# A four-layer graph network on one core: plain, relational and graph layers put into one program per engine, their first products taken tile by tile

## The chip, the cores and the metric

The kernel runs on one core of one Trainium2 chip. The metric is the device time of one launch in microseconds. The core has five instruction streams: TensorE (PE, matrix products; PEld is its weight load), VectorE (DVE), ScalarE (ACT), GpSimd (POOL) and SyncE (SP, which here only issues transfers). They meet through semaphores. PEclk is the TensorE clock that was granted, as a share of 2.4 GHz.

## The reference, cut to what matters

A graph of 3125 nodes and 100000 edges, 128 features a node, goes through four blocks. Ahead of each stands a layer norm with relu, behind each a residual sum.

```
h = relu(layernorm(x)); x += L0(h): relational max over incoming edges, relu
h = relu(layernorm(x)); x += L1(h): relu(bn((h + sum of h[src]) @ W1)) @ W2, relu     (the "plain" layer)
h = relu(layernorm(x)); x += L2(h): twice  out = sum over edges of (h @ W[rel])[src] + h @ loop_w + b
h = relu(layernorm(x)); x += L3(h): h @ W_in + b_in, then four times
        t = h @ Wc[i]; agg = sum of t[src] * norm + bc[i]; h = layernorm(h + relu(agg)) * g + b
```

## The kernel before, in words

The nodes are 25 tiles of 128. The first stage (until 1213 us of the profile) computes L0 and beside it counts the edges into adjacency matrices, in 8 bits: one plain matrix (25 strips of 400 KB) and one split by relation (32 halves of 1600 KB). From then on the edge sums are matrix products of such a strip with the node rows. The rows are cut into a high and a low 16-bit part, so each (tile, strip) pair costs two products. A "cut" is such a pair of parts: `g.zcut` lies in the tile Z, `g.cut` in the tile cut.

After it come three blocks. Each is a `nc.Block()` with one program for each engine, and at its end the engines meet in a barrier:

- `isomorphism_layer`, the plain layer. Five rounds of five tiles. A round is 100 products on PE (line 1269: 50 of 384 columns, 50 of 256), the hidden product (line 1287) and the second product (line 1299). DVE and ACT normalise the round and write its cut (`GroupNorm`, lines 832 to 860; its semaphore `s_cut` rises by 2 a round). SP loads the plain strips, then the first four relational halves, and stores each round's cut to the DRAM table from which POOL gathers (line 1229).
- `relational_layers`, two passes of 32 halves. On PE a half is 50 products of 512 columns (`dense`, line 1853), in between lie the gathered sums (`few`, line 1835) for the nine sparse tiles and the tile products (`tile`, line 1811). POOL gathers rows for `few` (line 1575). SP issues seven parameter loads at the start (line 1581), then the halves (line 1589), each when its slot is free, then the plain strips 0 to 19 (line 1593). DVE waits for all seven transfers and reduces them to statistics (lines 1674 to 1679). PE transposes these (line 1865) between its first and its second half. The last pass makes the inputs of the graph layers tile by tile, in an order called `order`: `again` (line 1820, a transpose) and `enter` (line 1825, the product with W_in) lag two tiles behind, so two of each stand after the loop. DVE ends it with the cut of the last tile (line 1664).
- `graph_layers`, four layers of five rounds. A round is again 100 products (line 1269) and five products with the weights (line 1299); DVE normalises. SP loads the weights (line 1429) and the last five strips (line 1431). PE and DVE begin when the weights have landed (lines 1447 and 1498).

The order of work is written out by hand in each engine's program; each queue runs its own instructions in that order.

Of the kernel before, what the change touches and what calls it, by code (L numbers as in the profile page):

```python
# [23 lines left out]
ALU = mybir.AluOpType  # L24
# [1208 lines left out]
class Sums:  # L1233
# [24 lines left out]

    def tensor(self, e, i, cut, weights, base=0, parts_of=None):

        g, n = self.g, base * (2 * TROUNDS)

        def sums(q, tiles):
            last, (lo, hi) = None, self.parts[q]
            for a in tiles:
                adj = g.arena[:, i * TILES * NT * P // 4:(i + 1) * TILES * NT * P // 4].bitcast(F8).rearrange(
                    "p (k a n) -> p k a n", k=TILES, a=NT)[:, lo:hi, a, :]
                for part in range(2):
                    last = e.matmul(self.sums(i, q), cut[:, a, part, :], adj, start=a + part == 0,  # L1269
                                    stop=a + part == NT)  # L1270
            return last
# [7 lines left out]
        for q, (lo, hi) in enumerate(self.parts):  # L1279
# [3 lines left out]
            sums(q, range(NT - TILES, NT) if i == 0 and parts_of else range(NT)).then_inc(self.s_sum, 1)  # L1283
        for q, (lo, hi) in enumerate(self.parts):
# [53 lines left out]
def isomorphism_layer(g):  # L1338
# [7 lines left out]
    with g.nc.Block() as block:  # L1346
        @block.gpsimd
        def _(e):
            e.sem_inc(m.s_go, 1)

        @block.sync
        def _(e):
            load_adjacency(g, e, s_ld)

            def half(k):
                e.wait_ge(m.s_sum, 2 * ((4 * k + 3) // TILES + 1))
                e.dma_start(*load_half(g, k, k)).then_inc(s_half[k], 16)

            def rows(r):
                e.wait_ge(norm.s_cut, 2 * (r + 1))  # L1360
                store_cut(g, e, g.zcut, r, s_row)
            half(0)
            rows(0)
            half(1)
            rows(1)
            half(2)
            rows(2)
            half(3)
            rows(3)
            rows(4)  # L1370

        @block.vector
        def _(e):
            step = Chain(e, s_c)
            batch_norm_vector(g, e, step, s_v, s_r)
            for i in range(TROUNDS):
                for q, (lo, hi) in enumerate(m.parts):
# [12 lines left out]
        def _(e):  # L1390
            batch_norm_scalar(g, e, s_v, s_r)
            for i in range(TROUNDS):
                m.scalar(e, i, 1.0 / (scale * COUNT))
                norm.scalar(e, i)
# [766 lines left out]
```

## Time and profile before

| | us |
|---|---|
| median of three runs | 2650.6 (2649.99 to 2651.94) |
| the profiled execution | 2652.58, span 2650.7 |
| PE busy | 1977.3 (75%) |
| DVE busy | 1328.0 (50%) |
| POOL busy | 1490.7 (56%) |
| ACT busy | 670.7 (25%) |
| mean granted clock of PE | 0.808 |
| plain layer | 1214.6 to 1308.3 |
| relational layers | 1308.7 to 2321.4 |
| graph layers | 2321.9 to 2640.6 |

The spans of the layers are from the first to the last instruction of each in the timeline. In 40 equal slices of the span (66 us each), PE and its clock read:

```profile
PE   6744545555554545436899999998999999799996
PEclk8855655656565655568999999999999999899998
```

A digit is a tenth of a slice. From the 20th slice on PE is busy nearly all the time at full clock; the dip near the end is where the relational layers end and the graph layers begin.

### The profile page before, as it was taken

The page shows a single profiled execution, that of the slowest core. Times are in us where ns is not written, and L with a number is a line of the kernel's source. Part 1 is how long each engine was busy: PE and PEld are TensorE (multiplying, and loading weights), DVE is VectorE, ACT ScalarE, POOL GpSimd, SP SyncE. Part 2 cuts the span into 40 slices and gives each one's busy share as a digit, 9 for nine tenths or more (in the row PEclk, how much of TensorE's full clock was granted, in tenths as well). Part 3 has the DMA queues.
Part 4 walks back from the last instruction along what each step waited for, and adds up shares of the span by engine and source line. Part 5 has one row for each costly group of instructions (what it writes and reads, how often), then busy time and mean ns, then how long its engine had stood idle before and what let it go on. Part 6 is the DMA issues. An engine that isn't in the chain of part 4 may idle for free. (4 is left out here: it accounts for less than half of the span.)

```text
span 2650.7 us, 33489 instructions
## 1 busy us (share of the span) xinstructions
PE 1977.3 (75%) x11712; PEld 1095.3 (41%) x11712; DVE 1328.0 (50%) x3186; ACT 670.7 (25%) x1332; POOL 1490.7 (56%) x1528
## 2 busy tenths in 40 slices
PE   6744545555554545436899999998999999799996
PEld 3411111111121111124555555554555555467775
DVE  6466666666666666654322222221323332357775
ACT  4244445445454444424200000000000000100000
POOL 4277777777777777760156666663576657400000
PEclk8855655656565655568999999999999999899998
DMA  5545555555555555564354454465444444610000
GB/s 177 184 130 159 168 166 160 172 157 162 157 162 156 162 165 168 156 203 166 129 172 160 148 171 150 150 144 144 163 149 161 131 161 147 104 40 1 1 6 21
DMA packets 183331, 370.18 MB, mean 140 GB/s; under 512 B 38760, under 2 KB 119254, under 8 KB 174838
## 3 DMA queue, kind: packets, MB, share of 16 engines
q1 hardware_dynamic: 129208, 263.74, 28.1%
q0 software_dynamic: 48704, 101.21, 16.4%
q10 hardware_dynamic: 5246, 3.03, 0.4%
q8 instruction: 96, 1.57, 0.2%
q14 instruction: 77, 0.63, 0.1%
HBM read 232.54 MB, written 135.28 MB: 139 GB/s over the span
## 5 line engine op out<-in xcount | busy, mean ns | idle before, releaser
L925 POOL DMA_INDIRECT arena<-table_rel,key_rel x784 | 789.0, 1006 | 278.0 <-issue 233.6
L1053 PE MATMUL ps_out<-arena 128*128 128x400 f16 x1024 | 380.4, 509 | 438.2 <-DVE arena L959 396.6
L1097 ACT ACTIVATE arena<-ps_out 128x800 fp8e4<-128x800 f32 x512 | 400.2, 834 | 437.1 <-PE ps_out L1053 436.9
L1575 POOL DMA_INDIRECT arena<-table_cut,src_at x324 | 312.6, 965 | 277.2 <-DMA table_cut<-Z 111.7
L943 DVE SCALAR_TENSOR_TENSOR arena<-arena,keep_max 128x128 f32<-128x128 f32 x784 | 275.3, 351 | 328.5 <-DMA arena<-table_rel,key_rel 318.6
L1575 POOL DMA_INDIRECT arena<-table_next,src_at x324 | 314.9, 972 | 186.6 <-issue 91.8
L1053 PEld LDWEIGHTS ps_out<-arena 128*128 128x128 f16 x1024 | 85.3, 117 | 656.4 <-DVE arena L959 409.6
L1853 PE MATMUL ps_out<-arena,Z 128*128 128x512 fp8e4 x1600 | 352.3, 380 | 0.0
L1853 PE MATMUL ps_out<-arena,cut 128*128 128x512 fp8e4 x1600 | 350.2, 379 | 0.0
L959 DVE TENSOR_TENSOR arena<-iota,arena 128x1072 f16<-128x1072 f16 (+1 forms) x384 | 271.5, 707 | 0.0
L1269 PE MATMUL ps_out<-arena,cut 128*128 128x384 fp8e4 (+1 forms) x1500 | 207.9, 300 | 45.3 <-PEq L116 43.5
L1853 PEld LDWEIGHTS ps_out<-arena,Z 128*128 128x128 f16 x1600 | 156.8, 98 | 183.6 <-issue 2.2
L1853 PEld LDWEIGHTS ps_out<-arena,cut 128*128 128x128 f16 x1600 | 156.5, 98 | 182.7
L1835 PE MATMUL ps_out<-arena 128*128 128x256 f16 x1296 | 166.1, 283 | 34.5 <-issue 26.3
L1269 PEld LDWEIGHTS ps_out<-arena,cut 128*128 128x128 f16 x1500 | 147.1, 98 | 103.7 <-issue 47.5
L1835 PEld LDWEIGHTS ps_out<-arena 128*128 128x128 f16 x1296 | 127.5, 99 | 68.5 <-issue 28.5
L1040 PE MATMUL ps_t<-arena 128*128 128x50 f16 x1568 | 96.6, 212 | 77.7 <-DVE arena L953 77.7
L1617 DVE TENSOR_SCALAR CS<-ps_out,unit 128x512 f32<-128x512 f32 x32 | 24.0, 751 | 256.8 <-PE ps_out L1853 256.8
L1617 DVE TENSOR_SCALAR CS<-ps_out 128x512 f32<-128x512 f32 x32 | 22.1, 692 | 260.1 <-PE ps_out L1853 260.1
L1040 PEld LDWEIGHTS ps_t<-arena 128*128 128x128 f16 x1568 | 87.6, 118 | 139.2 <-DVE arena L953 92.1
L1269 PE MATMUL ps_out<-arena,Z 128*128 128x384 fp8e4 (+1 forms) x1000 | 139.5, 302 | 7.2 <-DMA w<-in_L_gnn_bc 6.3
L1777 ACT ACTIVATE tT<-ps_t 128x128 f32<-128x128 f32 x50 | 13.4, 268 | 517.9 <-PE ps_t L1785 517.9
(312 smaller groups left out, 1993.8 us busy)
## 6 DMA issues: line engine op xcount, KB each, us to landing
arena<-adjacency SPq DMA_DIRECT2D x64, 1600.0 KB, 7.0
adjacency<-arena SPq DMA_DIRECT2D x160, 320.0 KB
running_rows<-arena SPq DMA_DIRECT2D x392, 128.0 KB
arena<-adjacency_plain SPq DMA_DIRECT2D x50, 400.0 KB, 9.4
table_rel<-arena SPq DMA_DIRECT2D x25, 512.0 KB, 2.9
arena<-table_rel,key_rel POOLq DMA_INDIRECT x784, 2.9
adjacency_plain<-adj SPq DMA_DIRECT2D x50, 128.0 KB, 2.5
arena<-table_cut,src_at POOLq DMA_INDIRECT x324
```

The costliest lines, as they stand in the source:

```text
L925: e.indirect_dma_start(message(t), None, table, bass.IndirectOffsetOnAxis(key[:, t:t + 1], 0)).then_inc(s_msg[t % both], 16)
L943: e.scalar_tensor_tensor(fold(t), fold(t - 1), g.keep_max[:, t:t + 1], message(t), ALU.add, ALU.max).then_inc(s_run, 1)
L959: e.tensor_tensor(*onehot(g.hot_spot, b % 2, first, end, g.spot, b)).then_inc(s_spot, 1)
L1040: e.matmul(out[:, :, w * WIN:(w + 1) * WIN], g.hot_low[:, q % 2, w // 2, :, w % 2], g.hot_flat[:, q % 2, w // 2, :, w % 2].rearrange("p (a ...
L1053: last = e.matmul(g.ps_out[:, u % 2, x * 512:x * 512 + KW], g.hot_low[:, q % 2, k, :, x], g.hot_spot[:, b % 2, k, :, x], start=True, stop= ...
L1097: e.activation(g.half[h % 2].rearrange("p (a w x) -> p a w x", a=NT, x=R * WIN)[:, :, at:at + 2, :], g.ps_out[:, u % 2, 0:1024].rearrange( ...
L1269: last = e.matmul(self.sums(i, q), cut[:, a, part, :], adj, start=a + part == 0, stop=a + part == NT)
L1575: e.indirect_dma_start(g.picked[:, w % 2 * BLOCKS + k, :, :].rearrange("p a f -> p (a f)"), None, tables[y], bass.IndirectOffsetOnAxis(g.s ...
L1617: e.tensor_scalar(rows[:, k % 2, :, h * HD:(h + 1) * HD].rearrange("p r (w n) -> p r w n", n=WIN), g.ps_out[:, h, 0:512].rearrange("p (w r ...
L1777: e.activation(g.tT[:, i % 2, :], g.ps_t[:, i % 2, 0:P], ACT.Copy).then_inc(s_hT, 1)
L1835: last = e.matmul(g.ps_out[:, w % 2, 1024:1024 + CODES], g.picked[:, w % 2 * BLOCKS + k, part, :], g.hot_code[:, w % 2, k // 2, :, k % 2], ...
L1853: last = e.matmul(g.ps_out[:, h, 0:512], cuts[y][:, a, part, :], adj[:, a, :], start=x + part == 0, stop=x + part == NT)
```

## The change

The three blocks become one block with one program per engine. `isomorphism_layer` and `graph_layers` no longer open blocks; they return their four programs (SP, DVE, ACT, PE), and `later_layers` (formerly `relational_layers`) calls the plain layer's ahead of its own and the graph layers' behind it. Waits on semaphores stand where the meetings were:

- PE: the plain layer, then `dense(0, 0)`, which now waits for each round's cut (`norm.s_cut`) before the first product on that round's tiles. The first transpose `turn(0)`, which wrote a bank that the plain layer used, moves behind it. The order of the rest of the passes stays.
- PE, end of the second pass: the 50 products of the first graph round's first part (384 columns) are made in `early`, in the tile order `order`, each waiting for that tile's cut (`s_late`), between the two last `again` and the two last `enter`; then the 50 of 256 columns. `products` is the rest of the round, split from `tensor`.
- SP: the relational parameters wait for the plain layer's last product, behind that layer's last store. The graph weights wait for the last tile product, the last five strips for the last gathered sum.
- DVE waits for the plain layer's last sums before it writes `codes` over the strips; ACT waits for the plain layer's last rows; POOL needs only the five stores, as before.

```diff
+    def add(self, e, i, q, cut, tiles, begin, end):
+        g, last, (lo, hi) = self.g, None, self.parts[q]
+        for x, a in enumerate(tiles):
+            ...
+            for part in range(2):
+                last = e.matmul(self.sums(i, q), cut[:, a, part, :], adj, start=begin and x + part == 0,
+                                stop=end and x + part == len(tiles))
+        return last
...
-def graph_layers(g, a, out, s_plain):
+def graph_layers(g, a, out, s_plain, s_p, s_sum):
...
+    def sync(e):
+        e.wait_ge(s_p, 2 * NT)
+        for part in params:
+            e.dma_start(*part).then_inc(s_par, 16)
+        e.wait_ge(s_sum, 2 * GATHERED)
+        for k in range(NT - TILES, NT):
+            e.dma_start(g.slot(k, NT * P, U8), g.adjacency1[k]).then_inc(s_last, 16)
...
             for i in range(TROUNDS):
+                if n == 0 and i == 0:
+                    e.wait_ge(s_par, 16 * len(params))
+                    m.products(e, 0, g.w9[:, 0:D])
+                    continue
...
         @block.sync
         def _(e):
+            before[0](e)
+            e.wait_ge(iso.s_prod, 2 * TROUNDS)
             for part in params:
                 e.dma_start(*part).then_inc(s_par, 16)
...
+            behind[0](e)
...
         @block.vector
         def _(e):
+            before[1](e)
...
+            e.wait_ge(iso.s_sum, 2 * TROUNDS)
             codes(0, 0)
...
+            behind[1](e)
         @block.scalar
         def _(e):
+            before[2](e)
+            e.wait_ge(norm.s_h, NT)
             e.wait_ge(s_deg, 1)
...
                 for x, a in enumerate(order if y and m == 0 else range(NT)):
                     if y and m == 0:
                         e.wait_ge(s_ready, x + 1)
+                    elif m == 0 and a % TILES == 0:
+                        e.wait_ge(norm.s_cut, 2 * (a // TILES + 1))
...
-            turn(0)
+            before[3](e)
             for y in range(2):
                 for m in range(HALVES + 1):
                     if m < HALVES:
                         dense(y, m)
                     if y == 0 and m == 0:
+                        e.wait_ge(iso.s_read, 2 * TROUNDS)
+                        turn(0)
                         e.wait_ge(s_stat, 1)
...
-            for i in range(NT, NT + 2):
-                again(i)
-                enter(i)
-    return s_plain
+            def early(lo, hi):
+                for x in range(lo, hi):
+                    e.wait_ge(s_late, x + 1)
+                    done = last.add(e, 0, 0, g.zcut, order[x:x + 1], x == 0, x == NT - 1)
+                return done
+            e.wait_ge(s_ev, 2 * HALVES)
+            e.wait_ge(s_plain[0], 64)
+            e.wait_ge(s_plain[1], 64)
+            early(0, 10)
+            again(NT)
+            early(10, 14)
+            enter(NT)
+            early(14, 18)
+            again(NT + 1)
+            early(18, NT - 2)
+            enter(NT + 1)
+            early(NT - 2, NT).then_inc(last.s_sum, 1)
+            e.wait_ge(s_o2, NT)
+            last.add(e, 0, 1, g.zcut, order, True, True).then_inc(last.s_sum, 1)
+            behind[3](e)
```

First place, PE from the plain layer's last products (1299 before, 1306 now) to the second half of the first pass (1853 before, 1865 now). Before:

```order
L1299 MATMUL ps_t<-w,CS 128x128 x5
L1346 UNCONDITIONAL_BRANCH
L1779 UNCONDITIONAL_BRANCH
L1785 MATMUL ps_t<-ident,tin 128x128
L1853 MATMUL ps_out<-arena,Z 128x512 x50
L1865 MATMUL ps_out<-ident,stat 1x128 x3
L1853 MATMUL ps_out<-arena,Z 128x512 x50
```

And now:

```order
L1306 MATMUL ps_t<-w,CS 128x128 x5
L1865 MATMUL ps_out<-arena,Z 128x512 x50
L1795 MATMUL ps_t<-ident,tin 128x128
L1879 MATMUL ps_out<-ident,stat 1x128 x3
L1865 MATMUL ps_out<-arena,Z 128x512 x50
```

The first 50 products follow the plain layer with no meeting between; the transpose of tin moved behind them; the three transposes of stat keep their place ahead of the second 50.

Second place, PE from the last tile product of the second pass (1811 before, 1821 now) to the first weights product of the graph layers (1299 before, 1306 now). Before:

```order
L1811 MATMUL ps_out<-w,tT 128x128
L1825 MATMUL ps_out<-tH 128x128
L1820 MATMUL ps_out<-ident,CS 128x128
L1825 MATMUL ps_out<-tH 128x128
L1820 MATMUL ps_out<-ident,CS 128x128
L1825 MATMUL ps_out<-tH 128x128
L1562 UNCONDITIONAL_BRANCH
L1496 UNCONDITIONAL_BRANCH
L1269 MATMUL ps_out<-arena,Z 128x384 x50
L1269 MATMUL ps_out<-arena,Z 128x256 x50
L1299 MATMUL ps_t<-w,CS 128x128 x5
```

And now:

```order
L1821 MATMUL ps_out<-w,tT 128x128
L1835 MATMUL ps_out<-tH 128x128
L1265 MATMUL ps_out<-arena,Z 128x384 x20
L1830 MATMUL ps_out<-ident,CS 128x128
L1265 MATMUL ps_out<-arena,Z 128x384 x8
L1835 MATMUL ps_out<-tH 128x128
L1265 MATMUL ps_out<-arena,Z 128x384 x8
L1830 MATMUL ps_out<-ident,CS 128x128
L1265 MATMUL ps_out<-arena,Z 128x384 x10
L1835 MATMUL ps_out<-tH 128x128
L1265 MATMUL ps_out<-arena,Z 128x384 x4
L1265 MATMUL ps_out<-arena,Z 128x256 x50
```

The 50 products of 384 columns now stand among the last `again` (1820, now 1830) and `enter` (1825, now 1835), and only the last four are behind the last `enter`.

Third place, SP around the parameter loads. Before:

```order
L1229 DMA table_cut<-Z 128x5x256 x2
L1346 UNCONDITIONAL_BRANCH
L1578 UNCONDITIONAL_BRANCH
L1581 DMA w<-in_L_gnn_W 128x8x128
```

And now:

```order
L1229 DMA table_cut<-Z 128x5x256 x2
L1584 DMA w<-in_L_gnn_W 128x8x128
```

The loads stay behind the store of the last round's cut.

## Rows read from the trace of the kernel before

**Rows 1.** The chain that ended last, in order of time: start, duration, what.
```profile
2321.83 0.05 issue
...
2322.31 4.22 DMA w<-in_L_gnn_bc
...
2326.57 15.63 PE ps_out L1269 x100
...
2343.57 13.58 PE ps_out L1269 x100
```

**Rows 2.** Waits of PE, 1322 to 2289 us: total, times, longest.
```profile
PE ps_out L1835 <- issue: 14.6, 5, 7.6
PE ps_out L1835 <- DVE arena L1606: 8.2, 4, 2.7
```

**Rows 3.** Timeline at the first meeting: start, duration, instruction, [idle before, releaser].
```profile
1297.12 1.38 PE L1299 MATMUL ps_t<-w,CS 128*128 128x128 f32 x10 [0.23 <-ACT CS L1316]
...
1309.46 0.48 PE L1785 MATMUL ps_t<-ident,tin 128*128 128x128 f32 x1 [10.96 <-ACT tin L1764]
...
1309.73 12.70 PE L1853 MATMUL ps_out<-arena,Z 128*128 128x512 fp8e4 x50
...
1313.61 31.50 SPq L1589 DMA_DIRECT2D arena<-adjacency  x4
...
1319.56 1.35 DVE L1675 TENSOR_REDUCE stat<-w 128x1 f32<-128x1152 f32 x1 [7.26 <-DMA bias<-in_L_gnn_ln_b]
...
1321.16 0.29 DVE L1677 TENSOR_REDUCE stat<-tH 128x1 f32<-128x128 f32 x1
...
1322.27 0.49 PE L1865 MATMUL ps_out<-ident,stat 128*1 128x128 f32 x3
...
1322.59 10.96 PE L1853 MATMUL ps_out<-arena,Z 128*128 128x512 fp8e4 x50
```

**Rows 4.** The SP queue of its own at the first meeting.
```profile
1307.96 0.37 SPq L1229 DMA_DIRECT2D table_cut<-Z  x1
1308.73 0.37 SPq L1581 DMA_DIRECT2D w<-in_L_gnn_W  x1
```

**Rows 5.** Stretches: busy time and count by engine, granted clock, DMA share, GB/s.
```profile
1290.00:1300.00 10.00, 8.27 (x66) 6.59 (x63) 3.26 (x6) 2.04 (x4) 0.00 (x0) 1.00 0.11 33
1305.00:1310.00 5.00, 0.54 (x2) 0.36 (x3) 2.87 (x7) 1.67 (x7) 0.00 (x0) 0.50 0.22 60
...
2305.00:2309.00 4.00, 3.98 (x18) 2.40 (x18) 0.00 (x0) 0.00 (x0) 0.00 (x0) 0.50 0.27 107
2309.00:2313.00 4.00, 3.37 (x16) 3.37 (x17) 0.48 (x1) 0.66 (x3) 0.00 (x0) 0.50 0.01 4
2313.00:2316.00 3.00, 0.95 (x7) 0.76 (x6) 1.80 (x9) 0.59 (x2) 0.00 (x0) 0.94 0.00 0
```

**Rows 6.** Transfers issued 1308 to 1322 us: count, KB, us to landing.
```profile
arena<-adjacency SPq DMA_DIRECT2D x1, 1600.0 KB, 10.7
...
bias<-in_L_gnn_ln_g SPq DMA_DIRECT2D x1, 256.0 KB, 5.3
bias<-in_L_gnn_ln_b SPq DMA_DIRECT2D x1, 256.0 KB, 6.4
```

**Rows 7.** Timeline at the second meeting.
```profile
2304.98 4.00 PE L1835 MATMUL ps_out<-arena 128*128 128x256 f16 x18 [11.06 <-issue]
...
2313.56 0.39 PE L1825 MATMUL ps_out<-tH 128*128 128x128 f32 x2
...
2316.16 0.33 PE L1820 MATMUL ps_out<-ident,CS 128*128 128x128 f32 x1 [2.21 <-ACT CS L1749]
...
2318.10 0.49 ACT L1749 ACTIVATE CS<-X,small,inv_dev 128x128 f32<-128x128 f32 x1 [0.43 <-DVE small L1657]
...
2319.49 0.79 PE L1825 MATMUL ps_out<-tH 128*128 128x128 f32 x2 [0.37 <-ACT tH L1755]
...
2321.03 0.35 DVE L1664 SCALAR_TENSOR_TENSOR Z<-H,dsc,Z 128x128 f16<-128x128 f32 x1
```

More of the change, by code:

```diff
@@ L1283, in tensor, with products @@
             sums(q, range(NT - TILES, NT) if i == 0 and parts_of else range(NT)).then_inc(self.s_sum, 1)
+        self.products(e, i, weights, base)
+    def products(self, e, i, weights, base=0):
+        n = base * (2 * TROUNDS)
         for q, (lo, hi) in enumerate(self.parts):
@@ L1403, in isomorphism_layer, with half, rows @@
-    return s_row, s_half
-def graph_layers(g, a, out, s_plain):
+    def sync(e):
+        load_adjacency(g, e, s_ld)
+        def half(k):
+            e.wait_ge(m.s_sum, 2 * ((4 * k + 3) // TILES + 1))
+            e.dma_start(*load_half(g, k, k)).then_inc(s_half[k], 16)
+        def rows(r):
+            e.wait_ge(norm.s_cut, 2 * (r + 1))
+            store_cut(g, e, g.zcut, r, s_row)
+        half(0)
+        rows(0)
+        half(1)
+        rows(1)
+        half(2)
+        rows(2)
+        half(3)
+        rows(3)
+        rows(4)
@@ new lines, in vector @@
+    def vector(e):
+        step = Chain(e, s_c)
+        batch_norm_vector(g, e, step, s_v, s_r)
+        for i in range(TROUNDS):
+            for q, (lo, hi) in enumerate(m.parts):
+                at = slice(i * TILES + lo, i * TILES + hi)
+                e.wait_ge(m.s_prod, 2 * i + q + 1)
+                e.tensor_tensor(g.Y[:, at, :], m.out(q).rearrange("p (k f) -> p k f", f=D),
+                                g.rows[:, 0, :].unsqueeze(1).to_broadcast([P, hi - lo, D]),
+                                ALU.add).then_inc(m.s_read, 1)
+                e.wait_ge(m.s_read, 2 * i + q + 1)
+                step(e.scalar_tensor_tensor(g.X[:, at, :], g.Y[:, at, :], 0.0, g.X[:, at, :], ALU.max, ALU.add))
+            norm.moments(e, i, step)
+            norm.spread(e, i, step)
+            norm.cuts(e, i)
@@ new lines, in scalar, with tensor @@
+    def scalar(e):
+        batch_norm_scalar(g, e, s_v, s_r)
+        for i in range(TROUNDS):
+            m.scalar(e, i, 1.0 / (scale * COUNT))
+            norm.scalar(e, i)
+    def tensor(e):
+        for i in range(TROUNDS):
+            if i >= EARLY_ROUNDS:
+                e.wait_ge(s_ld[i], 16 * TILES)
+            e.sem_inc(m.s_go, 1)
+            m.tensor(e, i, g.cut, g.w9[:, D:2 * D])
+    return m, norm, s_row, s_half, (sync, vector, scalar, tensor)
+def graph_layers(g, a, out, s_plain, s_p, s_sum):
@@ L1516, in relational_layers, with later_layers @@
+    return m, (sync, vector, scalar, tensor)
+def later_layers(g, a, out):
     nc = g.nc
@@ L1557, in relational_layers @@
     job = {n: i for i, n in enumerate(order)}
+    last, behind = graph_layers(g, a, out, s_plain, s_p, s_sum)
     def bank(k):
@@ L1564, in _ @@
         def _(e):
+            e.sem_inc(iso.s_go, 1)
             e.wait_ge(s_row, 16 * TROUNDS)
```

227 lines of the change are left out of this document (79 added, 148 removed).

## The prediction

> **What bounds the kernel now.** I read the two PE lines of the page first, then the chain of waits, then the waits of PE, then the timeline of all engines around the two places where the blocks meet, with the granted clock beside it. The chain [rows 1] starts at 2321.83 us, at the start of the graph layers: the two weight loads (until 2326.53), then PE through four layers (a round's 100 products 13.58 us, the first 15.63). It cannot be followed past the meeting, so what stands before must be asked for by stretch. From the first meeting to the last relational half PE is idle for only some 23 us of 967, nearly all ahead of the gathered sums [rows 2]. POOL's next gather waits for the gathered sum two before it, so POOL follows PE there and does not set a pace of its own. So from 1309 to 2289 us everything hangs on when PE goes through its list; a shift of PE at the first meeting goes through rigidly to the end, and so does one at the second.
>
> At the first meeting PE ends the plain layer at 1298.50 and stands idle for 10.96 us, since ACT and DVE still normalise the last round [rows 3]. That round's cut is ready just before SP stores it at 1307.96 [rows 4]. Then the first half takes 12.70 us where the second takes 10.96, because the clock had fallen: 1.00 from 1290 to 1300, 0.50 from 1305 to 1310 [rows 3, 5]; that is 2.4 and 1.2 GHz. At the second meeting PE ends the last tile at 2313.95, does four small steps of the last two tiles with idle time between, and stands until 2326.57 [rows 1, 7].
>
> **Part one, the first meeting: what the products gain and what comes late next.** Fifty products cost 10.96 us at full clock, 0.219 each [rows 3]. The tiles of rounds 0 to 3 are ready when PE ends at 1298.50, so 40 products run at once, to 1307.3, at full clock since PE does not pause. The last ten wait for the cut at about 1307.95 and end at 1310.2. Before, this half ended at 1322.43. That is 12.2 us earlier.
>
> But the next thing on PE's list is the three transposes of the statistics, and they wait for DVE (1321.45, the end of line 1677), which waits for the last of SP's seven parameter loads, seen at 1319.56 [rows 3]. Those loads stand on SP behind the store of the last cut, both in the old order and in the new. That store is issued at 1307.96 and takes 0.37, so the loads start at 1308.33 and not at 1308.73 [rows 4]: 0.4 us is all they gain. DVE has its codes done long before and waits either way. So the transposes can begin at 1321.05 and PE idles from about 1310.5 to there. The wait for the statistics takes the place of the wait for the cut.
>
> And the cold start moves with it. Idle time of 10.96 us brought the clock to 0.50; so will 10.6. From the first transpose to the end of the second half was 11.28 us warm (1322.27 to 1333.55). A cold start costs 1.74 (12.70 less 10.96) [rows 3] or 2.05 (15.63 less 13.58) [rows 1]; I take 2.0, since it now covers the transposes too, and 0.1 for the semaphore. The second half ends at 1321.05 + 0.1 + 11.28 + 2.0 = 1334.4 where it ended at 1333.55. The first meeting's removal costs 0.9 us.
>
> Bounds. Below: if the clock had come back by the time of the transposes, 1321.15 + 11.28 = 1332.4, a gain of 1.1. Above: the second of the four half loads in the row at 1313.61 waits only for the first half's products, so it is now issued at once behind the first of them, where it used to wait until 1322.4. It then shares the transfer engines with the parameters. With one such load behind it, the last parameter took 6.4 us to land, the one before it 5.3 [rows 6]. A second load of the kind adds at the nearest row 1.1, and at the worst the parameters land with the end of a half: 10.7 less 6.4, 4.3 us more. I take 0, because both halves are issued behind the parameters on one queue, and keep 4.3 for the range. The Trainium skill says (DMA: Bandwidth & Descriptors, "Queues, rings and completion order") that on each transfer engine the descriptors of one queue are consumed in ring order; by that rule a later load of SP cannot be served ahead of a parameter and the addition is 0. The row leaves it open: 6.4 against 5.3 may be order alone.
>
> The other edits there cost nothing on the path: turn(0) (0.27 to 0.48 us) lies in PE's idle time; the codes of DVE and the root of ACT come up to 0.8 earlier and wait for others; POOL begins, as before, when the fifth store has landed, and its first gathered sum is used only behind the third half.
>
> **Part two, the second meeting.** PE is free at 2313.95 [rows 7]. Rates: 13.58 us for 50 x 384 + 50 x 256 = 32000 columns [rows 1], so a product of 384 columns is 0.163 us and one of 256 is 0.109. The clock is back to 0.94 from 2313 to 2316 [rows 5], after 8 us of work at 0.50 since 2304.98, and PE now has no pause that would take it away. Step by step: 20 products, 3.26, to 2317.2; the last but one transpose (its input was ready before 2316.16) 0.1; 8 products, 1.30, to 2318.6; enter 0.2; 8 products to 2320.1. ACT and DVE need from the end of the transpose (2316.49) to the end of the last hn (2318.59) 2.1 us, so hn stands at 2319.5 and the last transpose does not wait: 2320.3. Ten products, 1.63, to 2321.9; the last enter, 0.2 and a drain, to about 2322.4. The cut of the last tile follows an enter by 1.1 us (2320.28 to 2321.38) [rows 7], so at 2323.5 the last two products can go, PE having idled 1 us: 2324.0. Then 50 of 256 columns, 5.43: 2329.4. Before, the same 100 products ended at 2342.20 [rows 1]. The second meeting's removal gains 12.8 us.
>
> What hides the rest: the graph weights are issued at 2313.8 and land 4.7 us later (2321.83 to 2326.53 in rows 1), at 2318.5, and are wanted at 2329.4; the last five strips are wanted only in the fifth round; strips 0 to 9, which the early products wait for, are issued while the last three halves still run. The waits on every tile cost PE nothing where the tile is there. From then on the rounds are the same instructions, and the end shifts as the first round does.
>
> Bounds: if PE ran all 100 products at the low clock they would take 13.58 more, and the gain would be a loss of 0.8; if the last tile did not hold PE up it would be 13.8.
>
> **Sum.** +0.9 - 12.8 = -11.9. The profiled execution's span 2650.7 would be 2638.8 and its own time 2652.58, 2640.7. The median of the runs shown is 2.0 below that execution, so in its terms 2650.6 - 11.9 = 2638.7.
>
> **Rivals.**
> - *Both meetings pay.* If the statistics were not late, the first meeting would give its 12.2 us too: 2650.6 - 12.2 - 12.8 = 2625.6. For it speaks that PE's idle time there is as large as at the second. Against it speaks the order on SP and the DVE row that starts at 1319.56 on the last parameter. Chance 0.04.
> - *The early half delays the parameters.* As worked out above, 1.1 to 4.3 more: 2639.8 to 2643.0. For it: 6.4 after 5.3. Against: one queue, issued later. Chance 0.14.
> - *The clock comes back late at one of the two places*, by as much as after 2304.98, where PE worked 8 us at 0.50, against the 4 that a loss of 2.0 stands for. One such case costs 2 us more, 2640.7; both 2642.7; both and the worst of the rival before 2647.0. Chance 0.08.
> - *Slower: the low clock holds on after the new idle time.* Place: the restart at 1321. Price: half of the time that PE works at the low clock. The gain of 11.9 already pays 2.0 for it, so it is used up when the loss there reaches 13.9, some 28 us at 0.50, and slower by 0.2% at about 38 us. With 40 us: 2638.7 + 18 = 2656.7. For it: the same engine at 2304.98 needed twice the usual time. Against: no row shows more than 8 us. Chance 0.03. The Trainium skill (TensorE: Matmul & The Clock Gate, "Seeing it yourself") warns that the gate has been seen stuck low for over 50 us; no row here shows that.
> - *The change doesn't do what it says*: some wait in the tail (a strip, the tile order) holds the early products until the old place. Then 2650.6 + 0.9 = 2651.5. Against: every wait there was traced above. Chance 0.03.
>
> **How the numbers follow.** The forecast has 0.68; 2638.7, its own range 2636.5 to 2640.8. The range 2635 to 2643.5 adds the delay of the parameters and one late clock, and leaves out the two ends. No change means within 0.2%, 2645.3 to 2655.9, about what this kernel's runs can tell. Faster: the forecast, the first rival, the second, nearly all of the third: 0.92. Same: 0.05. Slower: 0.03.
>
> **What will show it.** First half: 40 products straight behind the plain layer's last, at full clock, end near 1310. Then PE idle for 10 to 11 us until the transposes of stat, which come no earlier than 1320.5, with DVE waiting on the last parameter load; the second half at about 12.5 us. The rest of the relational passes 0.5 to 1.5 us later than before, shape unchanged. In the tail some 50 products between 2314 and 2325, the weights product near 2330, and 308 us from there to the end of the span, as before (2650.7 less 2342.2). I am wrong in step one if the transposes come before 1318 or the parameters land past 1322; in step two if PE's clock is 0.50 after 2316 or if the last four products of 384 columns start past 2325.

## The result, and the profile after

| | us |
|---|---|
| kernel before, median of 9 runs | 2651.63 (2642.70 to 2654.97) |
| changed kernel, median of 9 runs | 2639.28 (2633.66 to 2646.49) |
| ratio | 0.9958, 95% interval 0.9945 to 0.9972 |
| profiled execution of the changed kernel | 2639.28, span 2637.5 |

The change makes the kernel faster by 0.42%: 11.1 us by the ratio, 12.4 by the medians, 13.3 by the two profiled executions (2652.58 and 2639.28). A ratio here and below leaves out the few executions that fell into a slower state of the chip, while a median takes all. The forecast was 2638.7. The sum came out, but partly by luck: one of its two terms was too small a price, and something that was not in the sum paid for it.

To see that, the two spans are cut at events that both traces have. Each number is the distance between two rows. There is one such trace of the kernel before, and single executions of one kernel lie up to 13 us apart, so a difference of a microsecond or two in a stretch that the change does not touch means little.

| from, to | before | after | difference | forecast |
|---|---|---|---|---|
| start to the plain layer's first instruction | 1214.63 | 1214.87 | +0.24 | 0 |
| plain layer, to PE's last product in it | 83.87 | 84.62 | +0.75 | 0 |
| first meeting, to the end of the second half | 35.05 | 37.44 | +2.39 | +0.9 |
| relational passes, to the end of the last half | 955.1 | 952.6 | -2.5 | 0 |
| last half to the last tile product | 25.08 | 23.97 | -1.1 | 0 |
| last tile product to the first weights product | 28.32 | 15.25 | -13.07 | -12.8 |
| graph layers to the end | 308.66 | 308.76 | +0.10 | 0 |

**First meeting.** The timeline of PE in the changed kernel; columns as in [rows 3]: start, duration, instruction, then in brackets the idle time before it and who ended it.

```profile
1299.32 8.80 PE L1865 MATMUL ps_out<-arena,Z 128*128 128x512 fp8e4 x40
1308.97 2.33 PE L1865 MATMUL ps_out<-arena,Z 128*128 128x512 fp8e4 x10 [0.85 <-DVE Z L845]
1311.14 0.27 PE L1795 MATMUL ps_t<-ident,tin 128*128 128x128 f32 x1
1322.73 0.80 PE L1879 MATMUL ps_out<-ident,stat 128*1 128x128 f32 x3 [11.31 <-DVE stat L1682]
1323.32 13.61 PE L1865 MATMUL ps_out<-arena,Z 128*128 128x512 fp8e4 x50
```

Where [rows 3] have 10.96 us of nothing and then 50 products, 40 products now follow with no pause, ten more wait 0.85 us for the cut, and the half is over at 1311.30. Then PE waits 11.31 us for `stat`. The wait has kept its length and changed its name: DVE where ACT stood. The same stretch from DVE and from SP:

```profile
1308.94 0.37 SPq L1229 DMA_DIRECT2D table_cut<-Z  x1
1309.36 0.53 SPq L1584 DMA_DIRECT2D w<-in_L_gnn_W  x1
...
1312.65 0.43 SPq L1584 DMA_DIRECT2D bias<-in_L_gnn_ln_b  x1
...
1320.78 1.35 DVE L1680 TENSOR_REDUCE stat<-w 128x1 f32<-128x1152 f32 x1 [8.43 <-DMA bias<-in_L_gnn_ln_b]
...
1322.39 0.28 DVE L1682 TENSOR_REDUCE stat<-tH 128x1 f32<-128x128 f32 x1
```

The name behind the arrow is the cause: the last parameter load, issued behind the store of the last cut as in [rows 4]. A "cold start" is what PE loses because its clock has fallen while it idled. The granted clock by stretch (columns as in [rows 5]) shows where it went:

```profile
1305.00:1310.00 5.00, 4.14 (x20) 1.72 (x19) 2.87 (x8) 2.46 (x7) 0.00 (x0) 1.00 0.02 7
1310.00:1316.00 6.00, 1.42 (x8) 0.53 (x5) 2.35 (x8) 0.47 (x2) 2.99 (x4) 0.92 0.70 181
1316.00:1320.00 4.00, 0.00 (x0) 0.00 (x0) 0.00 (x0) 0.00 (x0) 3.08 (x4) 0.50 0.75 285
1320.00:1325.00 5.00, 2.27 (x7) 0.95 (x8) 3.94 (x11) 0.00 (x0) 3.78 (x5) 0.50 1.00 396
1325.00:1330.00 5.00, 5.00 (x16) 1.91 (x15) 0.14 (x1) 0.00 (x0) 3.78 (x5) 0.63 0.81 304
```

PE, idle, is granted 0.50, that is 1.2 GHz, in both stretches from 1316 to 1325, and 0.63 is the mean of the next one, which has both levels in it; from 1330 to 1337 the granted clock is 1.00. The second half takes 13.61 us, where it took 10.96 warm.

**Second meeting.** The timeline from the last gathered sum on: PE's rows, with DVE's last cut and SP's load of the weights between. The last tile product ends at 2313.49.

```profile
2306.09 4.00 PE L1845 MATMUL ps_out<-arena 128*128 128x256 f16 x18 [11.27 <-issue]
...
2310.93 2.33 PE L1821 MATMUL ps_out<-w,CS 128*128 128x128 f32 x16
...
2313.52 0.38 SPq L1423 DMA_DIRECT2D w<-in_L_gnn_Wc  x1
...
2313.55 3.41 PE L1265 MATMUL ps_out<-arena,Z 128*128 128x384 fp8e4 x20
...
2321.47 0.38 PE L1835 MATMUL ps_out<-tH 128*128 128x128 f32 x2
...
2322.53 0.35 DVE L1669 SCALAR_TENSOR_TENSOR Z<-H,dsc,Z 128x128 f16<-128x128 f32 x1
...
2322.95 5.96 PE L1265 MATMUL ps_out<-arena,Z 128*128 128x384 fp8e4 x52 [0.77 <-DVE Z L1669]
...
2328.74 1.52 PE L1306 MATMUL ps_t<-w,CS 128*128 128x128 f32 x10
```

[Rows 7] have the four small steps alone, with idle time between, and [rows 1] the 100 products behind a wait for the weights. Now 48 of the products fill the gaps (20, 8, 8, 10 and 2), the only wait left is 0.77 us for the last cut, and the first weights product starts at 2328.74. The forecast's 2329.4 left out its own first term; with it, it is 2330.3. The weights, issued at 2313.52, are no longer waited for.

**In between.** PE's waits from 1337 to 2289 us (total, times, longest), to be held against [rows 2]:

```profile
PE ps_out L1845 <- issue: 14.8, 6, 7.0
PE ps_out L1845 <- DVE arena L1611: 5.4, 3, 2.2
```

The second row seems to say that one wait for DVE has gone. The timelines show that it has not. Both kernels wait over 1 us at the same seven gathered sums; at the first of them the wait fell from 2.69 to 1.47 us and is now put down to "issue". The seven together fell from 21.96 to 19.46 us. That is the 2.5 us by which the relational passes became shorter.

### The profile page after: what moved, and what is told of

Read it like the earlier page. It is cut to its first block, busy times and chain, and to the rows that moved or that the text cites. A ratio compares the mean times of both kernels' runs of the same rounds, so it can differ in the third digit from the quotient of the medians.

```text
span 2637.5 us, 33454 instructions
## 1 busy us (share of the span) xinstructions
PE 1968.0 (75%) x11712; PEld 1093.0 (41%) x11712; DVE 1326.8 (50%) x3186; ACT 670.4 (25%) x1332; POOL 1486.4 (56%) x1528
## 4 chain that ended last, share of the span: by engine, by line
PE 49%; DVE 3%; issue 1%; ACT 0%; DMA 0%; SPq 0%; ACTq 0%
PE ps_out L1865 26%; PE ps_out L1265 12%; PE ps_out L1845 6%; PE ps_out L1821 4%; PE ps_t L1306 1%; DMA bias<-in_L_gnn_ln_b 0%; DVE arena L1611 0%; PE ps_t L1795 0%; PE ps_out L1835 0%; ACT CS L1323 0%; DVE H L1466 0%; DVE H L1467 0%; DVE CS L1456 0%; DVE H L1468 0%; DVE CS L1460 0%
## 5 line engine op out<-in xcount | busy, mean ns | idle before, releaser
L950 DVE TENSOR_TENSOR arena<-iota,arena 128x1024 f16<-128x1024 f16 x196 | 134.5, 686 | 16.6 <-PE ps_out L1053 16.2
```

The lines of the kernel that those rows point to most:

```text
L950: e.tensor_tensor(*onehot(g.hot_low, q % 2, 0, P, g.low, order[q], 1)).then_inc(s_low, 1)
```

## The experiments

Twelve kernels ran, in three sets: nine new ones, two of these a second time, and the changed kernel once more. Each set has its own runs of the kernel before on the same chip, and ratios are to those. Chip 15 gave 2650.47 us for it (11 runs), like the runs above. Chips 9 and 11 gave 2935.39 (25 runs) and 2964.13 (35 runs); what differs there is told under the last heading. Times are therefore compared within a set. Between sets only intervals are compared, and of these the last column alone reads the same on all chips where the tail is the same (15.24 or 15.25 us). The changed kernel itself ran on chip 11 but not on chips 9 and 15.

| kernel | chip | median us | ratio, 95% | first meeting | last tile product to weights product |
|---|---|---|---|---|---|
| changed, first runs | | 2639.28 | 0.9958 (0.9945 to 0.9972) | 37.44 | 15.25 |
| t_lateprod | 9 | 2918.86 | 0.9937 (0.9910 to 0.9965) | 35.78 | 22.53 |
| h_latefirst | 9 | 2928.15 | 0.9954 (0.9927 to 0.9981) | 43.0 | 15.25 |
| h_hold5 | 9 | 2910.51 | 0.9895 (0.9862 to 0.9929) | 36.91 | 15.24 |
| h_warm | 9 | 2918.39 | 0.9953 (0.9918 to 0.9987) | 41.2 | 15.24 |
| all_four | 15 | 2615.41 | 0.9867 (0.9846 to 0.9887) | 23.05 | 15.13 |
| h_params | 15 | 2619.65 | 0.9892 (0.9872 to 0.9912) | 23.06 | 15.25 |
| t_hold2 | 15 | 2631.05 | 0.9937 (0.9917 to 0.9956) | 35.79 | 15.24 |
| t_gap | 15 | 2631.26 | 0.9938 (0.9918 to 0.9958) | 35.13 | 15.46 |
| after_again | 11 | 2944.54 | 0.9933 (0.9898 to 0.9968) | 38.14 | 15.24 |
| h_latefirst2 | 11 | 2942.04 | 0.9932 (0.9896 to 0.9967) | 43.8 | 15.24 |
| h_warm2 | 11 | 2947.46 | 0.9951 (0.9914 to 0.9988) | 41.2 | 15.24 |
| t_serial | 11 | 2954.84 | 0.9969 (0.9933 to 1.0004) | 38.6 | 29.31 |

### What the second meeting's gain is made of: t_lateprod and t_serial

t_lateprod puts the 50 early products behind the small steps:

```diff
-            early(0, 10)
             again(NT)
-            early(10, 14)
             enter(NT)
-            early(14, 18)
             again(NT + 1)
-            early(18, NT - 2)
             enter(NT + 1)
-            early(NT - 2, NT).then_inc(last.s_sum, 1)
+            early(0, NT).then_inc(last.s_sum, 1)
```

> The changed kernel with one part undone: in the tail all 50 products of 384 columns stand behind the last again and enter; no meeting returns. Theory (the gain of the second place has two parts, products under the small steps and no meeting): the four small steps take 6.3 us from the last tile as in the kernel before, then 50 products, 8.2 us, then 5.4; the first weights product comes 5 to 7 us later after the last tile product than in the changed kernel (20 to 22 us instead of 15.0); 5 to 7 us slower than the changed kernel, 0.9975 of the kernel before. Rival A (the meeting and its weight loads were all of it): same as the changed kernel. Rival B (only the products under the steps pay): as slow as the tail before, 12.8 us more.

The small steps have their idle time back (2.41, 1.24 and the like), and PE's timeline reads:

```profile
2592.66 0.30 PE L1830 MATMUL ps_out<-ident,CS 128*128 128x128 f32 x1 [2.41 <-ACT CS L1758]
...
2595.89 0.79 PE L1835 MATMUL ps_out<-tH 128*128 128x128 f32 x2 [0.37 <-ACT tH L1764]
2596.48 16.25 PE L1265 MATMUL ps_out<-arena,Z 128*128 128x384 fp8e4 x100
2612.56 1.52 PE L1306 MATMUL ps_t<-w,CS 128*128 128x128 f32 x10
```

The interval is 22.53 us for 15.25: the products between the small steps bring 7.3. That is a little over what was expected (5 to 7), since the clock has fallen during the small steps and the 100 products take 16.25, not 13.58. So 2.7 of the 7.3 us are the clock's.

t_serial does this too, and SP loads the weights only when the last cut stands, with PE waiting for them. That is the old order of events without a meeting:

```diff
     def sync(e):
-        e.wait_ge(s_p, 2 * NT)
+        e.wait_ge(s_late, NT)
...
+            e.wait_ge(last.s_par, 32)
+            early(0, NT).then_inc(last.s_sum, 1)
```

> The edit of t_lateprod, and the graph weights are loaded only when the last cut is made and PE waits for them before its first graph product: the kernel before's tail without the meeting itself. Theory (the meeting itself is 0.5 us; what it cost was the order it forced: weights behind the last cut and no product under the small steps): last tile product to first weights product 27.5 to 28 us, where the kernel before had 28.3 and t_lateprod 22.5. Rival (barrier and branch cost several us by themselves): 23 to 25 us.

The timeline of PE and SP:

```profile
2604.01 0.80 PE L1835 MATMUL ps_out<-tH 128*128 128x128 f32 x2 [0.37 <-ACT tH L1764]
2605.87 0.38 SPq L1424 DMA_DIRECT2D w<-in_L_gnn_Wc  x1
...
2611.22 16.41 PE L1265 MATMUL ps_out<-arena,Z 128*128 128x384 fp8e4 x100 [6.41 <-DMA w<-in_L_gnn_bc]
2627.46 1.52 PE L1306 MATMUL ps_t<-w,CS 128*128 128x128 f32 x10
```

29.31 us, 6.8 more than t_lateprod and 1.0 more than before with its meeting (28.32). I had expected 27.5 to 28. Of that 1.0 us, 0.8 lies in the 100 products, which take 16.41 us for 15.63, both from a cold start; small steps and wait together take 0.2 more than before. So the gain has two parts of about the same size, the weights' transfer (6.8) and the filled gaps (7.3, with the warm clock), and the meeting itself costs nothing that these rows can show. The medians of the set agree: 2954.84 for t_serial, 2944.54 for the changed kernel. Its harm is only what it keeps in order.

### Do the early products pay at the first meeting: h_latefirst, h_latefirst2, after_again

```diff
-                    elif m == 0 and a % TILES == 0:
-                        e.wait_ge(norm.s_cut, 2 * (a // TILES + 1))
+                    elif m == 0 and a == 0:
+                        e.wait_ge(norm.s_cut, 2 * TROUNDS)
```

The first half waits for the last cut again. It ran in two sets; the second time beside the changed kernel itself (after_again).

> The changed kernel with one part undone: the first half of the first pass waits for all five cuts before its first product; no meeting returns. Theory (the early products only move the idle time and the cold start behind them): the first half runs cold from about 1309, 12.7 us, ends near 1321.7, the transposes follow within 1 us, the second half runs warm in 10.96 us; from the plain layer's end to the second half's end 34.5 to 35 us instead of 37.4, so 2.5 to 3 us faster than the changed kernel. Rival (early products pay at the first place): up to 12 us slower than the changed kernel.

> The edit of h_latefirst again (first half waits for all five cuts), since on the first chip PE paused inside the second half and its end could not be compared. Theory (early products only move the idle time and the cold start behind them): first half cold, 13 us, second half warm in 10.96; plain layer's end to second half's end 35 to 36 us, 0 to 3 us less than the changed kernel in the same set. Rival (they pay): 12 us more.

> The changed kernel itself once more, to stand beside the others of this set on their chip. Both theories: 0.994 to 0.997 of the kernel before where PE is paced as in the first comparison; plain layer's end to second half's end 35 to 38 us, last tile product to first weights product 15.2 us.

PE's timeline in h_latefirst2:

```profile
1502.99 13.64 PE L1865 MATMUL ps_out<-arena,Z 128*128 128x512 fp8e4 x50 [9.58 <-DVE Z L845]
...
1517.30 0.49 PE L1879 MATMUL ps_out<-ident,stat 128*1 128x128 f32 x3 [0.55 <-DVE stat L1682]
1517.62 7.36 PE L1865 MATMUL ps_out<-arena,Z 128*128 128x512 fp8e4 x32
1526.48 0.38 PE L1865 MATMUL ps_out<-arena,Z 128*128 128x512 fp8e4 x1 [1.50 <-issue]
```

The cold start is back in the first half (13.64), the transposes are warm (0.49) and come 23.9 us after the plain layer's end, where after_again has 22.8. The ratios are 0.9932 and 0.9933: undoing the early half changes nothing that can be measured. The twelve times of each kernel spread over some 40 us, so this speaks against a gain of 12 us (the rival) but can't tell the 0 to 3 us of the theory from nothing. That the early half brings nothing while `stat` is late rests on the place of the transposes, which moved by 1.1 us only. What the trace would say of the end of the second half can't be read here: PE pauses 1 to 2 us at a time in it, with no releaser but "issue" (last row). With the pauses, and the clock that falls in them (mean 0.59 from 1530 to 1537 us), the half takes 18.2 us in h_latefirst and 19.6 in this run, not 10.96.

### Is it the sixth half's load that makes the parameters late: h_hold5

```diff
                 if mt >= TILES:
-                    e.wait_ge(s_mm, mt - TILES + 1)
+                    e.wait_ge(s_mm, max(2, mt - TILES + 1))
```

> The changed kernel with the sixth half's load held until the second half's products are done; nothing else. Theory (that load, which the early products release, slows the parameters): the last parameter lands 6.4 us after its issue again instead of 8.1, the transposes of the statistics come 1.7 us earlier, 1.7 us faster than the changed kernel. Rival (one queue keeps its order, so a later load takes nothing): landing stays 8 us, no change.

The trace of the changed kernel tempts one to this theory: from its issue the last parameter took 6.4 us before [rows 6] and 8.1 after. With the load held until the second half is done it still took 7.6. The first of the seven issues and the end of DVE's wait for the last:

```profile
1500.60 0.53 SPq L1584 DMA_DIRECT2D w<-in_L_gnn_W  x1
...
1511.52 1.35 DVE L1680 TENSOR_REDUCE stat<-w 128x1 f32<-128x1152 f32 x1 [7.93 <-DMA bias<-in_L_gnn_ln_b]
```

Counted from the *first* issue like this, the last one landed after 10.9 us here. The eight traces that have the same order at this place and do not hold the load read 10.6 to 11.4 (11.42 in the first profile, 10.9 in t_lateprod on the same chip), and the kernel before 10.83. So holding the load changes nothing that stands out of this spread. SP now issues the group closer together (from the start of the first issue to the end of the last 3.7 us, before 4.8), so the last one waits longer for the ones ahead of it. The theory fell and the rival, one queue in order, stands. The ratio of this run, 0.9895, is lower than its neighbours'; its first meeting (36.9) gives no reason for it. Its relational passes do (1046 us, where the others of this set have 1050 to 1056). Whether the edit has a part in that, one trace can't say.

### The price of the cold start: h_warm, h_warm2

```diff
                         turn(0)
+                        e.wait_ge(s_half[1], 16)
+                        for k in range(46):
+                            e.matmul(g.ps_out[:, 1, 1024:1536], g.zcut[:, 0, 0, :], g.slot(1, R * NT * HD, F8)[:, 0:512],
+                                     start=k == 0, stop=k == 45)
                         e.wait_ge(s_stat, 1)
```

46 products whose result nobody reads keep PE at work while it waits for `stat`. The edit ran in two sets.

> The changed kernel with 46 more products of 512 columns, whose result nobody reads, in PE's idle time ahead of the statistics' transposes. Theory (the cold start costs 2.7 us in the second half and 0.3 in the transposes): the filler ends near 1321.5, ahead of the statistics, granted clock 1.00 throughout, transposes 0.5 us, second half 10.96 instead of 13.6; 2.9 us faster than the changed kernel. Rival (the half is slow for another reason, transfers beside it): 13.6 us stays, no change or 0 to 1 us slower by the filler.

> The edit of h_warm again (46 idle products ahead of the statistics' transposes), for the same reason. Theory (cold start is worth 1.3 to 2.9 us here): transposes 0.49, second half 10.96, plain layer's end to second half's end 34.5 us against 35.8 to 37.4 in the changed kernel. Rival: no difference.

PE's timeline in h_warm2, from the transposes on:

```profile
1531.78 0.49 PE L1883 MATMUL ps_out<-ident,stat 128*1 128x128 f32 x3 [0.56 <-issue]
1532.10 7.72 PE L1865 MATMUL ps_out<-arena,Z 128*128 128x512 fp8e4 x35
1541.89 0.38 PE L1865 MATMUL ps_out<-arena,Z 128*128 128x512 fp8e4 x1 [2.07 <-issue]
```

The clock was kept: transposes 0.49 where cold they take 0.80, 35 products in 7.72 us, 0.22 each. But then come the pauses again, and the half ends 41.2 us after the plain layer. No gain (0.9951 beside 0.9933, the intervals overlap), and no verdict on the price: what the warm clock saved can't be told from what the pauses cost. h_params gives warm halves without pauses instead.

### What bounds the first meeting: h_params

If `stat` is late because of the loads, loads that come earlier must give back PE's idle time and the cold start behind it. SP issues them behind the fourth store of the plain layer, before it waits for the fifth; the first two relations' weights share memory with the plain layer and so wait for its last product, still ahead of the fifth store. DVE does `statistics` ahead of `codes`.

```diff
         rows(3)
+        for part in early_params:
+            e.dma_start(*part).then_inc(s_par, 16)
+        e.wait_ge(m.s_prod, 2 * TROUNDS)
+        for part in late_params:
+            e.dma_start(*part).then_inc(s_par, 16)
         rows(4)
...
             e.wait_ge(iso.s_sum, 2 * TROUNDS)
+            statistics()
             codes(0, 0)
             codes(0, 1)
-            statistics()
```

> The changed kernel with the relational parameters loaded during the plain layer and the statistics ahead of the codes on DVE; the tail as in the changed kernel. Theory (the statistics are what keeps the first meeting's 12 us back): statistics end by 97 us after the plain layer's start instead of 107.8, PE goes from the first half into the transposes with no idle time over 1 us, clock 1.00, and from the plain layer's end to the second half's end it takes 23 us instead of 37.4: 14 us faster than the changed kernel. Rival (the first gathered sums are late instead, POOL starts no earlier): PE waits at the first gathered sum for up to 14 us and nothing is gained.

The timeline of DVE, SP and PE in it:

```profile
1302.78 1.34 DVE L1686 TENSOR_REDUCE stat<-w 128x1 f32<-128x1152 f32 x1
1302.81 0.38 SPq L1229 DMA_DIRECT2D table_cut<-Z  x1
1302.84 2.33 PE L1871 MATMUL ps_out<-arena,Z 128*128 128x512 fp8e4 x10 [0.86 <-DVE Z L845]
...
1305.11 0.49 PE L1885 MATMUL ps_out<-ident,stat 128*1 128x128 f32 x3
1305.44 10.96 PE L1871 MATMUL ps_out<-arena,Z 128*128 128x512 fp8e4 x50
```

DVE no longer waits for a transfer (no bracket in the first row), PE no longer waits for `stat`, no half is cold. The first meeting falls to 23.06 us, from 37.44 in the first profile and from 35.1 and 35.8 in the two kernels of this chip that leave it as it was (t_gap, t_hold2). The kernel falls to 2619.65, 0.9892 of the kernel before, and those two took 2631. The edit does two things, and they were not run apart: the codes that DVE now makes behind the statistics take 3.44 us, so with earlier loads alone the transposes would come some 3.4 us later, by an estimate from that duration. This is the first rival's gain, had by a second edit; the removal of the meeting alone could not give it.

### The gap ahead of the last gathered sum: t_gap, t_hold2, all_four

PE idles 11.27 us before `few` and comes out of it cold (4.00 us for 18 products that take 2.20 warm). t_gap puts 44 of the early products there:

```diff
+                    if y and m == HALVES:
+                        e.wait_ge(s_ev, 2 * HALVES)
+                        e.wait_ge(s_plain[0], 64)
+                        e.wait_ge(s_plain[1], 64)
+                        early(0, 22)
                     for w in after[m]:
```

t_hold2 holds the last eight plain strips back until the last gathered sum is done, in case they slow the gather:

```diff
                 e.wait_ge(s_mm, mt + 1)
+                if mt >= 2 * HALVES - 2:
+                    e.wait_ge(s_sum, 2 * GATHERED)
```

> The changed kernel with 44 of the 50 first products of the first graph round ahead of the last gathered sum, in PE's idle time there. Theory (the products are 7.2 us of work that the idle time hides, and they keep the clock up): the wait ahead of the last gathered sum is 7 us shorter, gathered sum and tile products run warm (2.2 and 2.2 us instead of 4.0 and 2.8), the tail ends with the chain of the last two tiles; 4 to 8 us faster than the changed kernel. Rival (the chain of the last tiles, 7.4 us, is the bound anyway): the products were hidden already, 0 to 2 us faster.

> The changed kernel with the last two groups of plain strips (eight of 400 KB) loaded behind the last gathered sum. Theory (the last gather lands 12 us and more after its last issue because those strips share the transfer engines): it lands within 4 us of its last issue, the last gathered sum does not wait 11.3 us but under 1, PE stays at full clock there, 10 to 14 us less from the last relational half to the first weights product; the second and third graph round may wait for strips up to 5 us. Rival (the gather is slow by itself): the wait stays, and the held strips cost up to 10 us more in the rounds.

PE in t_gap:

```profile
2286.01 7.31 PE L1265 MATMUL ps_out<-arena,Z 128*128 128x384 fp8e4 x44
2297.80 4.00 PE L1845 MATMUL ps_out<-arena 128*128 128x256 f16 x18 [4.48 <-issue]
```

44 products are hidden, but 4.48 us of idle time stay, `few` is as cold as ever, and later the small steps have nothing to fill them with. From the last half to the weights product it is 39.5 us, as without the edit (39.2): the rival's case, the products were hidden already. PE in t_hold2:

```profile
2298.94 3.44 PE L1847 MATMUL ps_out<-arena 128*128 128x256 f16 x18 [8.31 <-issue]
```

The wait falls to 8.31 us, where I had expected under 1, and that interval to 34.4. The ratios of both (0.9937 and 0.9938) lie beside the changed kernel's 0.9958 with intervals that overlap, so only the intervals in the trace tell them apart.

all_four joins h_params, t_gap and t_hold2.

> The changed kernel with four things added: the relational parameters are loaded during the plain layer (six transfers behind the fourth cut's store, the part of w that overlays the plain weights when these are read for the last time), the statistics stand ahead of the codes on DVE, 44 of the first graph round's products stand ahead of the last gathered sum, and the last two groups of plain strips are loaded behind that sum. Theory (each of the two idle places is a transfer that is late for a reason that the order of the lists sets): from the plain layer's end to the second half's end 23 us instead of 37.4, the last gathered sum waits under 1 us on the chip of the first comparison instead of 11.3, the tail from the last relational half to the first weights product 22 to 26 us instead of 39.2; 26 to 30 us faster than the changed kernel, 0.985 of the kernel before. Rival (the strips are wanted earlier than they land): the second graph round waits up to 10 us, which gives that part back; 16 to 20 us faster.

PE in the same place:

```profile
2278.61 7.31 PE L1265 MATMUL ps_out<-arena,Z 128*128 128x384 fp8e4 x44
2286.85 2.20 PE L1853 MATMUL ps_out<-arena 128*128 128x256 f16 x18 [0.93 <-issue]
```

Now the gap is closed: 0.93 us, and `few` is warm, 2.20. The interval is 32.8, 6.4 less than in the changed kernel, where t_gap alone gave nothing and t_hold2 4.8. It is short of what was expected of it, since the last two tiles' small steps (15.13 us to the weights product) are bare again. The first meeting takes 23.05. At 2615.41 us, 0.9867 of the kernel before, it is the fastest of all and beats both kernels; over h_params alone its intervals overlap. The rival, that held strips would come too late for the rounds, can be dropped: behind the first weights product PE waits for DVE alone in all_four and in t_hold2, as in the changed kernel, and the graph layers take 308.6 and 308.8 us.

## Why the prediction was right

**The order of events held.** 40 products straight behind the plain layer, end of the half at 1311.3 (forecast near 1310), PE idle for 11.31 us (10 to 11), transposes at 1322.73 (not before 1320.5), some 50 products in the tail, the weights product at 2328.74 (near 2330), 308.8 us from there to the end (308). Only the second half is off, 13.61 us for about 12.5. h_params shows that the parameters were indeed the bound of the first meeting, and t_serial that the second meeting's gain was, as worked out, transfer and gaps.

**The second term was right**, 12.8 against 13.07, and by its own steps: ten products more cost 1.62 us (20 took 3.41, ten 1.79), 0.162 each where the sum had 0.163, with 0.17 us on top for each group; the last cut done 1.0 us after its `enter` where it had 1.1.

**The first term was mis-sized**, +0.9 against +2.4. Two of its parts are off. The transposes start 23.24 us after the plain layer where the sum had 22.65: the loads began 0.4 earlier relative to it, as said, but landed 0.6 later from there (11.42 for 10.83), which is within the spread of the same order in other traces (10.6 to 11.4). And from the transposes to the end of the second half it took 14.20, where the sum had 13.28: the cold start cost 2.65 in the products and 0.31 in the transposes, 3.0 and not the 2.0 taken. The same place on chip 15 read 35.8 and 35.1 (second half 12.26 and 12.03, so 1.3 and 1.1 lost there), on average with the first 36.1, a term of +1.1 if the kernel before took its 35.05 there too, which no trace shows. The price of a cold start thus had no one value: 1.1, 1.3 and 2.65 in these three traces at one place, in the same instructions, where I drew 2.0 from two rows before.

**What the sum left out**: the relational passes, 2.5 us shorter, and the stretch ahead of the last tile product, 1.1 shorter, were forecast as rigid. In the latter the clock returned earlier: the 16 tile products at 2310.93 took 2.33 us, before 3.60. In the former the seven waits ahead of gathered sums became shorter. It is not a consequence of when PE comes to them: the passes took 951 to 953.5 in all four variants on chip 15, with PE 12 us earlier in two of them and not in the others. What let them run shorter stays open.

**The number was partly luck.** In the two profiles 1.5 us too little for the first meeting and 1.0 us in the stages ahead of it stand against 3.6 us that passes and last tile gave back and 0.3 us of the second term. The one claim of the prediction that did not hold is that a shift at the first meeting goes through rigidly. And with executions of the kernel before from 2642.70 to 2654.97, no forecast earns an agreement of 0.6 us.

**The rivals.** That the early half delays the parameters was put at 1.1 to 4.3 us; 0.6 came, no more than the spread, and h_hold5 shows no part of the sixth half's load in it. The prediction had said of 6.4 against 5.3 that the row "leaves it open"; counted from the first issue it looks like order alone. By the Trainium skill (DMA: Bandwidth & Descriptors, "Queues, rings and completion order") each transfer engine consumes the descriptors of one queue in ring order, though a later one may finish its write before an earlier one. h_hold5 agrees as far as it goes: 10.9 us without the later load, 10.9 with it in t_lateprod. The clock came back late, by 1 us and not by 2. It did not stick: a loss of 3.0 us is 6 us of work at half speed, and the remainder of the half ran at full clock. Both meetings pay, 2625.6, was not what this change does, but h_params reached 2619.65 with it. Some 5 us of that lie in the first stage, which no edit touches: in its profile the plain layer starts at 1209.4 us, not 1214.6.

## What to carry to other kernels

Before you take a barrier away, ask of each engine what it waits for next: here the idle time stayed 11 us and only its releaser changed from the cut to a parameter load, and the gain of 12 us came when that load was moved and what waited for it was put first, not when the barrier went. The barrier cost nothing by itself that could be seen; what it cost was the transfer and the small steps that it kept apart from the products, 7 us each. And two edits at one gap were worth nothing and 5 us alone, and 6 together, so read the idle time that is left after each.

## What the runs showed of the hardware that was not expected

**The three chips differed by more than any edit here.** The same kernel before took 2650 us on one chip and 2935 and 2964 on two others. Each was seen on one occasion, so the chip and the occasion can't be told apart. The difference has two places: the first stage ends 186 to 210 us later (the plain layer starts at 1400 to 1424 us, before at 1214.6), and the relational passes take 1046 to 1059 us for 951 to 955. Some of it comes back ahead of the last gathered sum, where PE waits 1.8 to 4.3 us and not 11.3. The graph layers take the same, 308.6 to 309.2. In the passes PE pauses. Its waits in after_again, 1525 to 2585 us:

```profile
PE ps_out L1865 <- issue: 25.0, 30, 1.7
PE ps_out L1821 <- issue: 20.2, 21, 2.1
PE ps_out L1835 <- ACT tH L1764: 14.8, 6, 8.5
```

The view that [rows 2] come from has neither of the first two. The profile names no releaser, and the cause is open. It has a consequence for reading: on such a chip a local gain can't be seen behind the pauses, as in h_warm, and an experiment that must be read to a microsecond is read from an interval without them, or on another chip.

**The gather's last rows are slow by themselves.** From the start of POOL's last gather instruction to the gathered sum it is 15.5 us in the changed kernel and 15.6 in t_gap. In t_hold2 and all_four, without the strips beside it, it is still 11.7 and 11.5. In t_hold2 no other queue moved anything from 2276 to 2300 us:

```profile
DMA packets 432, 0.85 MB, mean 36 GB/s; under 512 B 224, under 2 KB 224, under 8 KB 432
...
q0 software_dynamic: 432, 0.85, 81.9%
```

The time that these 432 packets took adds up to 81.9% of what 16 transfer engines have in 24 us, for 0.85 MB at 36 GB/s. All transfers of the first meeting together, most of them large, ran at 396 GB/s from 1320 to 1325 us. Holding the strips back is worth 3.8 of 15.5 us; the rest is the gather's own.
